# Block-diagonal queries, token-major experts, and a first FFN on rows sorted by expert

## The reference, cut to what matters

```
x = x + attn0(layernorm(x), ctx, ctx)     # 32 query heads of 8 on 8 key/value heads, 64 keys per batch
x = x + ffn0(layernorm(x), ...)           # 2 experts 256 -> 1024 -> 256, each row takes one of them
x = x + attn1(layernorm(x), ctx, ...)     # 16 heads of 16, keys and values widened from ctx, causal
x = x + ffn1(layernorm(x), ...)           # 256 -> 128, 8 experts of hidden 128..512 (top 2) and a shared one, -> 256

# ffn0
probs = softmax(x_flat @ w_router.T); top_idx = argmax(probs)
h = einsum('nd,ehd->enh', x_flat, w_fc)
a = square(where(h >= 0, h, 0.5 * h))
expert_out = einsum('enh,edh->end', a, w_proj)
out = einsum('end,en->nd', expert_out, mask * top_weight)   # only the chosen expert's row is kept

# ffn1, for k in the two largest gates and each expert e
acc = acc + (gelu(gelu(h * mask_e) @ w1 + b1) @ w2 + b2)     # a row with mask 0 gives a constant row per expert
out = out + acc * gate_k
```

## Time and profile before

| | |
|---|---|
| runs of the kernel, median (lowest, highest) | 390.66 us (390.49, 393.13) |
| the profiled execution's own time | 389.83 us |
| its span, first to last instruction | 387.8 us |
| PE busy | 345.8 us, 89% of the span |
| DVE, ACT, POOL busy | 163.6, 150.4, 90.8 us |

### The profile page before, as it was taken

The page is one execution under the profiler, slowest core; times in us unless marked ns, Lnnn a source line. Parts: engine busy times, 40 slices in busy tenths (PEclk is TensorE's granted clock), DMA queues, the critical chain, the costliest instruction groups (busy, mean ns, idle before and its releaser), DMA issues.

```text
span 387.8 us, 11733 instructions
## 1 busy us (share of the span) xinstructions
PE 345.8 (89%) x5105; PEld 282.2 (73%) x5105; DVE 163.6 (42%) x481; ACT 150.4 (39%) x349; POOL 90.8 (23%) x134
## 2 busy tenths in 40 slices
PE   2365679899998999899999999899999999996996
PEld 1234568777785887788788896788877888885784
DVE  4360473007730346088502684016364156327034
ACT  3012424332153332347142140433553666666452
POOL 6832423422342113142122430042100000200000
PEclk9999969989999999899999999999999999999899
DMA  3999000000000000000000000000000001000000
GB/s 87 288 401 365 8 1 3 3 3 2 0 3 3 3 3 2 3 3 3 0 5 3 0 1 2 5 0 2 0 2 27 3 1 32 0 0 15 14 1 29
DMA packets 7106, 12.84 MB, mean 33 GB/s; under 512 B 2576, under 2 KB 5392, under 8 KB 6288
## 3 DMA queue, kind: packets, MB, share of 16 engines
q1 hardware_dynamic: 7056, 12.10, 9.0%
HBM read 11.04 MB, written 1.05 MB: 31 GB/s over the span
## 4 chain that ended last, share of the span: by engine, by line
PE 82%; issue 6%; DVE 4%; SPq 3%; ACT 3%; POOL 1%; DMA 1%; DVEq 0%; POOLq 0%
PE Y L1243 27%; PE S L1243 27%; PE H L1243 24%; SPq L679 2%; PE S L1321 2%; DMA WKV<-in_wkv 1%; ACT PT L766 1%; PE S L1429 1%; PE S L1330 1%; POOL X L891 1%; SPq L674 1%; DVE XN L1002 0%; DVE MN L1030 0%; ACT YS L842 0%; PE S L1249 0%
## 5 line engine op out<-in xcount | busy, mean ns | idle before, releaser
L1243 PE MATMUL Y<-WP,A 128*128 128x256 f32 x256 | 64.0, 399 | 0.0
L1243 PE MATMUL H<-XT,WF 128*128 128x256 f32 x256 | 62.1, 391 | 0.0
L1243 PEld LDWEIGHTS Y<-WP,A 128*128 128x128 f32 x256 | 48.9, 199 | 8.1 <-issue 1.5
L1243 PEld LDWEIGHTS H<-XT,WF 128*128 128x128 f32 x256 | 47.9, 194 | 7.9 <-issue 1.5
L907 POOL TENSOR_TENSOR A<-R 128x512 f32<-128x512 f32 x32 | 33.2, 1040 | 61.9 <-PE Y L1243 57.5
L824 ACT ACTIVATE A<-H,B 128x256 f32<-128x256 f32 x84 | 35.6, 471 | 30.8 <-PE H L1243 30.7
L1243 PE MATMUL Y<-A,W 128*128 128x256 f32 x168 | 45.9, 383 | 0.4 <-DVE YG L1206 0.4
L1243 PE MATMUL H<-GH,W 128*128 128x256 f32 x168 | 44.6, 392 | 0.3 <-ACT GH L813 0.3
L796 ACT ACTIVATE R<-H 128x512 f32<-128x512 f32 x32 | 19.1, 598 | 47.4 <-POOL A L907 24.0
L1243 PEld LDWEIGHTS H<-GH,W 128*128 128x128 f32 x168 | 31.9, 195 | 5.7 <-issue 0.6
L1243 PEld LDWEIGHTS Y<-A,W 128*128 128x128 f32 x168 | 30.6, 192 | 6.3 <-issue 1.1
(11 more groups left out here) (171 smaller groups left out, 492.4 us busy)
## 6 DMA issues: line engine op xcount, KB each, us to landing
W<-in_w SPq DMA_DIRECT2D x2, 1344.0 KB, 9.2
WF<-in_wf SPq DMA_DIRECT2D x2, 1024.0 KB, 9.0
WP<-in_wp SPq DMA_DIRECT2D x2, 1024.0 KB, 11.1
X<-in_x SPq DMA_DIRECT2D x8, 128.0 KB, 7.5
out_dram<-X SPq DMA_DIRECT2D x8, 128.0 KB, 1.7
KR<-in_ctxT SPq DMA_DIRECT2D x4, 192.0 KB, 3.2
KR<-in_ctxT SPq DMA_DIRECT2D x8, 32.0 KB, 2.1
C<-in_ctx_in SPq DMA_DIRECT2D x1, 256.0 KB, 3.2
```

Of the source, the lines that this page charges most:

```text
L1243: return nc.tensor.matmul(o, a, b, start=start, stop=stop, skip_group_check=shared)
```

## The change

It does three things, and the tables of costs and urgencies are new, so that all five lists (SP has one now) are sorted anew.

**Block-diagonal queries.** In `p` the operands change places: the plain keys (`KR0`, `KT1`) are the stationary operand, and POOL builds four zero-padded copies of the queries (`queries0`, `queries1`), into the same tile `Z0` that held the padded keys, after the scores are done. The turned maxima are spread by DVE (`spread_shifts0`, `spread_shifts1`) to 8 x 128 columns instead of being copied by ACT. `p` is then 8 bfloat16 matmuls of 512 columns and 16 float32 ones of 256 in attention 0 (4 and 8 in attention 1). The padded keys of attention 1 move from DVE to POOL.

**Token-major experts.** FFN 1's down matmuls give rows on the partitions: two of 128 columns for each of 256 before. The gate is then a number per partition, and DVE adds expert times gate to `ACC` in two instructions, without ACT's copy and the gate-spreading matmul. What a masked row gives is added by one small matmul pair (`ROWS0`). `ACC` is turned by PE and copied by ACT before `widen`.

**Sorted rows.** FFN 0 runs in two sets of 512 rows (tiles 0 to 3, 4 to 7). When all gates of a set are known, PE forms prefix sums of the choice (`prefix`), DVE turns them into a slot for each row (`slots`), POOL scatters the normalised rows (computed again by `rows_again`) with 4 indirect DMAs to HBM, where the set has 5 tiles of 128 slots, and SP loads them back. The slots are 3 segments (256, 256 and 128 rows), each of one expert; SP reads the expert's number and loads its 2 MB of weights for each segment, into one of two buffers. Each segment is computed for its expert alone: 640 rows per set instead of 512 rows twice. The leaky unit is ACT (half) and DVE (maximum), the square stays on POOL. The results are stored to HBM by SP, gathered by POOL with an indirect DMA per tile, and added by DVE (`result_sorted`). Attention 1 of a tile starts from there. At the start, loads are fewer and larger, and ACT issues the first keys.

```diff
-BLOCKS0 = E0 * K0 // 2
+SETS = [[0, 1], [2, 3]]
+SET_SEGS = [[2] * len(groups) + [1] for groups in SETS]
...
+SET_PARTS = [[(j, i) for j, w in enumerate(segs) for i in range(K0 * w // 4)] for segs in SET_SEGS]
...
+            def expert_weights(n, j):
...
+                if j == 0:
+                    sp.wait_ge(experts_known, n + 1)
...
+                    filled(sp, "sort", m, "y", k)
+                e = sp.value_load(EXI[0:1, n, j:j + 1], min_val=0, max_val=E0 - 1)
+                sp.dma_start(WF0[:, q % 2, :, :], wf0[:, bass.ds(e, 1), :, :].rearrange("p e c h -> p (e c) h")
+                             ).then_inc(ld_seg[q], 16)
...
+            def sorted_rows(n, _):
+                sp.wait_ge(scattered[n], 16 * SET_TILES[n])
...
+            def results(n, j):
...
+                read_out(sp, "sort", n, "y", j)
+                sp.dma_start(results_sorted[n][2 * j * P:(2 * j + w) * P, :].rearrange("(k p) d -> p k d", p=P),
+                             YSB[n][:, 2 * j:2 * j + w, :]).then_inc(ys_stored[n], 16)
...
-            def leaky(g, i):
-                n = g * BLOCKS0 + i
-                b, done = filled(act, "ffn0", g, "u", i)
+            def half(m, i):
+                n = BLOCKS.index((m, i))
+                b, _ = filled(act, "sort", m, "u", i)
                 if n >= 2:
                     act.wait_ge(a0_ready, n - 1)
-                nc.scalar.activation(R0[:, n % 2, :], b[:, :], ACT.Prelu, alpha=0.5).then_inc(done, 1)
+                nc.scalar.activation(R0[:, n % 2, :], b[:, :], ACT.Copy, scale=0.5).then_inc(half_ready, 1)
...
+            def queries0(t, _):
+                filled(pool, "attn0", t, "h", 3)
+                for c in range(DC):
+                    nc.gpsimd.tensor_tensor(Z0[:, t % 2, c, :, :], QT0[:, t % 2, c, :].unsqueeze(1).to_broadcast([P, 4, P]),
+                                            quarter0[:, :].unsqueeze(2).to_broadcast([P, 4, P]), ALU.mult).then_inc(qz_ready, 1)
...
+            def scatter(n, _):
+                pool.wait_ge(slots_ready, n + 1)
+                for t in range(SET_TILES[n]):
+                    pool.wait_ge(xns_ready, SET_FIRST[n] + t + 1)
+                    pool.indirect_dma_start(rows_sorted[n][:, :], bass.IndirectOffsetOnAxis(ap=SLOT[:, n, t:t + 1], axis=0),
+                                            XNS[n][:, t, :], None).then_inc(scattered[n], 16)
+            def gather(n, t):
+                if t == 0:
+                    pool.wait_ge(ys_stored[n], 16 * len(SET_SEGS[n]))
+                pool.indirect_dma_start(YG0[n][:, t, :], None, results_sorted[n][:, :], bass.IndirectOffsetOnAxis(
+                    ap=SLOT[:, n, t:t + 1], axis=0)).then_inc(gathered[SET_FIRST[n] + t], 16)
...
+            def spread_shifts0(t, _):
+                b, done = filled(dve, "attn0", t, "t", 0)
+                nc.vector.tensor_tensor(MD0[:, t % 2, :, :], b[:, :].bitcast(bf16)[:, 0:P].unsqueeze(1).to_broadcast([P, 8, P]),
+                                        place[:, :].unsqueeze(2).to_broadcast([P, 8, P]), ALU.mult).then_inc(done, 1)
...
+            def larger(m, i):
+                n = BLOCKS.index((m, i))
+                dve.wait_ge(half_ready, n + 1)
+                b, done = filled(dve, "sort", m, "u", i)
+                nc.vector.tensor_tensor(R0[:, n % 2, :], R0[:, n % 2, :], b[:, :], ALU.max).then_inc(done, 1)
+            def rows_again(n, _):
...
+                for t in range(SET_TILES[n]):
+                    normed("ffn0", 0, 0, SET_FIRST[n] + t, XNS[n][:, t, :]).then_inc(xns_ready, 1)
...
+            def slots(n, _):
...
+                nc.vector.tensor_copy(EXI[:, n, 0:pairs + 1], EJ[:, 0:pairs + 1]).then_inc(experts_known, 1)
...
+                link(nc.vector.tensor_tensor(change, change, S16[:, n, 0:k], ALU.mult))
+                nc.vector.tensor_tensor(SLOT[:, n, 0:k], change, slot0, ALU.add).then_inc(slots_ready, 1)
...
+            def result_sorted(n, t):
+                row = SET_FIRST[n] + t
+                dve.wait_ge(gathered[row], 16)
+                nc.vector.scalar_tensor_tensor(X[:, row, :], YG0[n][:, t, :], TW[:, n, t:t + 1], X[:, row, :], ALU.mult, ALU.add
+                                               ).then_inc(taken, 1)
...
             def expert(g, j):
...
+                e = EXPERTS[j]
+                b, done = filled(dve, "ffn1", g, "y", j)
+                for k in range(2):
+                    ins = nc.vector.scalar_tensor_tensor(ACC[:, k, :], b[:, k * L:(k + 1) * L], gate[:, k, e:e + 1], ACC[:, k, :],
+                                                         ALU.mult, ALU.add)
+                    if k == 0 or j == E1:
+                        link(ins)
+                if j == E1:
+                    ins = nc.vector.tensor_tensor(flat(ACC[:, :, :]), b[:, GT:2 * GT], flat(ACC[:, :, :]), ALU.add)
...
             def probs0(t, _):
...
+                read_out(pe, "attn0", t, "t", 0)
+                pe.wait_ge(qz_ready, 2 * t + 2)
...
+                    pe.wait_ge(ofbank_ready, 3)
+                for k in range(2):
+                    for r in range(2):
+                        half = slice(r * S, (r + 1) * S)
+                        for bt in range(2):
+                            rows = slice(bt * S, (bt + 1) * S)
+                            mm(claims_[2 * r + k][0][rows, :], ofbank0[half, 2 * r + k, :], MD0[half, t % 2, :, rows], stop=False,
+                               shared=True)
+                for c in range(DC):
                     for i, (b, done) in enumerate(claims_):
                         quarter = slice(32 * i, 32 * i + 32)
                         for bt in range(2):
                             rows = slice(bt * S, (bt + 1) * S)
-                            ins = mm(b[rows, j * S:(j + 1) * S], KZ0[quarter, t % 2, c, r, rows], QT0[quarter, t % 2, c, rows],
-                                     start=False, shared=True)
-                        if j == 7:
+                            ins = mm(b[rows, 4 * c * S:4 * (c + 1) * S], KR0[quarter, c, t * P + bt * S:t * P + (bt + 1) * S],
+                                     Z0[quarter, t % 2, c, :, rows], start=False, shared=True)
+                        if c == DC - 1:
...
+            def up_sorted(n, i):
+                b, done = claim(pe, "sort", n, "u", i)
...
+                if part == 0:
+                    pe.wait_ge(ld_seg[q], 16 * 2)
+                    read_out(pe, "sort", n, "t", j)
+                w = P * SET_SEGS[n][j]
+                chunks = 512 // w
+                for c in range(chunks):
+                    ch = part * chunks + c
+                    for dc in range(DC):
+                        ins = mm(b[:, c * w:(c + 1) * w], WF0[:, q % 2, dc, ch * P:(ch + 1) * P], XTS[n][:, SEG_LIST.index((n, j)) % 2, dc, 0:w],
                                  start=(dc == 0), stop=(dc == DC - 1))
...
+            def down_sorted(n, i):
...
+                pe.wait_ge(a0_ready, block + 1)
+                w = P * SET_SEGS[n][j]
...
+                for k in range(SET_SEGS[n][j]):
+                    for c in range(chunks):
+                        ch = part * chunks + c
+                        ins = mm(at("sort", n, "y", j)[:, k * D:(k + 1) * D], hidden[:, c * w + k * P:c * w + (k + 1) * P],
+                                 WP0[:, q % 2, ch, :], start=(ch == 0 and k == 0),
+                                 stop=(ch == K0 - 1 and k == SET_SEGS[n][j] - 1), shared=True)
...
+            def turn_sums(g, _):
+                b, done = claim(pe, "ffn1", g, "k", 0)
+                read_out(pe, "ffn1", g, "y", E1)
+                for k in range(2):
+                    ins = nc.tensor.transpose(b[:, k * P:(k + 1) * P], ACC[:, k, :], identf[:, :])
...
-                ins = mm(at(*y)[:, 0:GT], W2[:, FIRST1[e] + c, :], A1[:, (g * NCH1 + i) % 4, :], start=(c == 0), stop=last_c)
+                for k in range(2):
+                    ins = mm(at(*y)[:, k * L:(k + 1) * L], A1[:, (g * NCH1 + i) % 4, k * P:(k + 1) * P], W2[:, FIRST1[e] + c, :],
+                             start=(c == k == 0), stop=last_c, shared=True)
...
-                    ins = mm(at(*y)[:, GT:2 * GT], selG[:, e, :], GTT[:, :])
+                if e == EXPERTS[-1]:
+                    read_out(pe, "ffn1", g, "g", 0)
+                    if g == 0:
+                        read_out(pe, "ffn1", 0, "z", 0)
+                    for k in range(2):
+                        ins = mm(at(*y)[:, (2 + k) * L:(3 + k) * L], GTT[:, k * P:(k + 1) * P], ROWS0[:, :], start=False, shared=True)
```

More of the change, by code:

```diff
@@ L145, in claims @@
     part, n, stage, i = s
[L146 to L147 removed]
+    if (part, stage) == ("sort", "d"):
+        j, i = SET_PARTS[n][i]
+        return [(part, n, "y", j)] if i == 0 else []
     if (part, stage) == ("ffn1", "w"):
@@ L294, in steps_and_needs @@
         ffn1(g)
-    first, last = {"ffn0": ("u", 0), "ffn1": ("c", 0)}, {"ffn0": ("d", BLOCKS0 - 1), "ffn1": ("o", 1)}
+    for n in range(len(SETS)):
+        sort(n)
```

(11 more changed lines are left out.)

696 lines of the change are left out of this document (411 added, 285 removed), and 47 rows, old and new, of the table URGENCY.

## The result

| | before | changed | forecast |
|---|---|---|---|
| median of the runs (lowest, highest) | 390.89 us (390.49, 393.13) | 375.8 us (374.74, 377.12) | 356 (338 to 380) |
| span of the profiled execution | 387.8 us | 374.4 us | 353.3 us |

The ratio is 0.960, 95% interval 0.955 to 0.965: faster by 4%, as forecast in sign, and inside the range, but 15 us where 35 were forecast. 20 us of the forecast's gain did not come.

What follows compares the result with a forecast made beforehand. PE's work plus its gaps was taken as the bound after the start. 387.8 - 42.2 - 2.3 - 6.2 + 3 + 10 + 2 + 1.2 = 353.3 us of span, a median of about 356, range 338 to 380.

Steps and rivals of the forecast that it cites:

- Later start: Start of the sorted first FFN: first up-projection at 88 against PE's 85, +3 us (bounds -15 and +18).
- PE's own bound: Before the first sorted up-projection: PE alone, with about 8 us more attention work, could start at 85 us.
- The way through HBM: From slots to first up-projection: four scatters, landing, reload, turning and copying, taken as 12.5 us.
- Removed expert: First FFN on PE: the equal of 320 records instead of 512, -42.2 us.
- `p` in wider matmuls: Attention's `p` on PE: 1.6 us a tile, 0.6 saved, and 0.14 a tile in attention 1; -2.3 us.
- The gaps in `p`: PE's waits ending as "issue" in or behind `p` should go with a tenth of the instructions: -6.2 us (bounds 0 and -6.2).
- The second set: PE's wait for the second set's rows, half clock after it, waits before attention 1 and handovers: +10 us (bounds 0, +25).
- Token-major experts: Second FFN: down products have as many columns as before, and DVE's multiply-adds go beside hidden work; put at nothing.
- A denser start: Rival: before the slots DVE keeps 88%, slots at 65, start 11 us earlier, 345 us; chance 0.17.
- The indirect DMAs hold POOL: Rival: each indirect DMA holds POOL longer than 1.2 us, deciding at 3.7; 5 gives 409 us; chance 0.09.
- DVE and POOL do stand in each other's way: Rival: DVE loses 10 us to POOL until the slots and another 7 after, 373 us; chance 0.18.
- The rival of the reload and the weights one behind the other: Rival: they serialise on SP's queue, both sets' starts and gathers late by 10 or more, 385 to 394 us; chance 0.04.

Runs made afterwards that it cites:

- e4: The changed kernel with DVE's spreading of the shifts cut to an eighth for tiles 2 to 5: 375.6 us.
- e5: The changed kernel with extra matmuls on PE, and the second segment's weights issued behind set one's reload: 365.8 us, ratio 0.933.
- e1: The changed kernel with about 112 extra bfloat16 matmuls, read by nobody, where PE waits between 46 and 103 us: 370.3 us, ratio 0.949.
- e8: The changed kernel with extra matmuls, set one's reload ahead of the second segment's weights, and the masked rows' sums moved into the second set's gap: 360.8 us, ratio 0.921.
- e12: The best version (e8) without its extra matmuls, both moves in the lists kept: 373.3 us, ratio 0.952.
- e9: The changed kernel without sorted rows: both experts for all rows in four groups, block-diagonal queries and token-major experts kept: 393.2 us, ratio 1.011.
- e6: The changed kernel without the weight loads of its last four segments: 368.6 us, ratio 0.941.
- e10: The changed kernel with only set one's reload moved ahead of the second segment's weights in SP's list, no extra matmuls: 375.7 us.

## Why the prediction was wrong

**The step that failed** is "Later start". It put the first sorted up-projection at 88 and its bound at 103; it came at 105. That is 17 of the 21 us by which the span missed (374.4 against 353.3).

- *The amount of work was right, the share was not.* Ahead of the slots 54.8 us of DVE's work were counted; the trace has 52.9 until 87. But the time was taken as DVE's work over a share between 62% and 88%, as if DVE alone set it. The share came out at 61%. Cutting 2.8 us of the work moved the slots by 0.4 (e4), and with PE's clock up 53.7 us of it were done by 79.1 (e5). What sets the slots is a chain that goes from PE to DVE or ACT and back for every tile, with nothing else in PE's list; PE's longest wait there, 2.96 us, is for one tile's maxima.
- *PE's own bound was taken at full clock.* The forecast put PE alone there at 85, from prices at full clock, though the half-clock block of the earlier trace rows had been priced elsewhere. With the FFN's matmuls gone from this stretch PE is busy 68% with gaps of up to 3.0 us, and it is granted 0.57 where the kernel before had 0.94 from 53 to 105. Extra matmuls give 6.3 us back (e1), and with the other two edits 12.5 (e8 against e12). That is the cause of the largest part, shown. The Trainium skill, "TensorE: Matmul & The Clock Gate", Part 1, says that the lower rate is the state of rest and activity releases it; the trace agrees (0.57, and 0.94 with the extra matmuls).
- *The way through HBM* was put at 12.5 us from slots to up-projection. It is 17.9, of which PE hides the end. With the clock up it is in the open, 3.5 us (e1), and it goes when the weights step behind the rows (e5), where the whole way takes 14.6. The forecast's 13.2 had the reload behind the weights, but not the scatter's landing as well.
- *What of the 17 us is accounted for.* The slots come 8.0 us earlier with the clock at 1.00 from 53 on (87.1 to 79.1, e5), and the way is 3.3 shorter with 2 MB of weights fewer ahead. The other 5.7 stay open: 3.1 in the slots (79.1 for 76), 2.1 in the way (14.6 for 12.5), and 0.5 that the forecast's own sum was over its 88 (76 + 12.5).
- *Removed expert:* right. 320 record equivalents; the starts of PE's timeline rows give 74.4 us for them against 119.7, so 45 saved where 42.2 were forecast.
- *`p` in wider matmuls:* 1.61 us a tile at full clock, forecast 1.6. In attention 1 it costs as much as before, 14.1 us in all by the starts, where 1.1 less were forecast.
- *The gaps in `p`:* "issue" is gone from the changed kernel's list of waits, as forecast. That the 6.2 us would be saved with it did not come, and this is the second term that failed. After 105 us PE's listed waits, without the second set's two, are 8.6 us; before they were 9.4, and 4.5 of these were "issue". Waits for DVE stand in their place, as in the unsorted kernel (e9).
- *The second set:* forecast 10, measured 1.6 + 4.1 and 1.0 at lower clock, 6.7 there, and no wait before attention 1's first turning, where 3.0 were forecast. From first up-projection to the end of the span 269.4 us against a forecast 265.3; with the gap closed (e8) 267.5.
- *Token-major experts:* put at nothing. The timeline's starts give 44.1 us for their matmuls, turned gates and sums against 41.7 before: 2.4 us on PE that were not in the sum, nearly all in the down products themselves (39.2 for 36.9). That is part of what is left over after the start; it was read, and not tried by itself.
- *The rivals.* A denser start did not come. The indirect DMAs hold POOL for 0.96 to 1.21 us; 1.2 was taken, and the point of 3.7 is far. DVE and POOL do stand in each other's way, but little; that the measured time lies at that rival's 373 us, in its band of 365 to 380 and so inside the stated range, is luck. The rival of the reload and the weights one behind the other has a part in it, but by 3.3 us at the first start and some 5 at the second, not 10 or more each. No rival had the clock in it.

DVE's timeline of the changed kernel shows a case of DVE and POOL in each other's way, one of the small slot operations:

```profile
84.06 1.10 DVE L1378 TENSOR_SCALAR EJ<-THR,N 128x2 f32<-128x2 f32 x1
```

POOL's timeline at that place, the building of padded keys:

```profile
83.10 2.04 POOL L1033 TENSOR_TENSOR Z<-KR,quarter 128x512 f32<-128x512 f32 x2 [6.61 <-PE S L1491]
```

An operation on two elements a partition takes 1.10 us and ends with POOL's, 0.02 us apart, where its neighbours take 0.16. Between 20 and 145 us nine of DVE's instructions take over half a us more than their like, some 7 us together, 4.4 of them ahead of the slots, where the rival had 17 and 10.

## What to carry to other kernels

Work that is taken out of a stretch may have been what kept PE's clock up and covered a chain of small steps there. Price the chain that is left at the lower clock, engine by engine in its own order, not by the busiest engine's share. And where rows go through HBM, count what loads stand ahead of them: for the reload those in its own queue, and for the landing those of other queues too (POOL's scatters landed late behind SP's weights). Put the data that is waited for first.

## What the runs showed of the hardware that had not been expected

- PE at 68% busy with no gap over 3.0 us was held near its lower clock for 50 us (0.57); 112 small matmuls (some 0.14 us each) in its gaps brought it to 0.94 and shortened the whole by 5.5 us.
- A scatter of 4 x 128 KB issued by POOL landed 2.4 us after its last issue with no weights on the way (e6), 4.4 to 5.5 behind 2 MB issued some 5 us before (e5, e8, e10, e12), 6.7 behind 2 MB and a store issued 1.4 to 2.2 us before, and 7.15 behind 4 MB.
- The same list of matmuls was granted 0.86 of the clock from 66 to 78 us in one execution (e1) and 1.00 in another (e5), and the slots came 1.7 us earlier in the second.
- Faults of order cover each other: the way through HBM was worth nothing by itself (375.7), 4.5 us with the clock up (370.3 to 365.8, with e5's better clock in it).
